# Token mixing in a four-stage network on one core: recurrence products moved to VectorE, key product split into high and low parts

## The reference

```python
xn = layer_norm(x, ln1_w, ln1_b); lx = time_shift(xn)
k = (xn * time_mix_k + lx * (1 - time_mix_k)) @ w_key      # v, r the same way
out = wkv(exp(time_decay), time_first, k, v)               # recurrence over time, per channel
x = x + out * sigmoid(r) @ w_output
xn2 = layer_norm(x, ln2_w, ln2_b); lx2 = time_shift(xn2)
fk = (xn2 * f_time_mix_k + lx2 * (1 - f_time_mix_k)) @ f_w_key      # 256 -> 1024
fr = (xn2 * f_time_mix_r + lx2 * (1 - f_time_mix_r)) @ f_w_recept
x = x + sigmoid(fr) * (square(relu(fk)) @ f_w_value)
```

## Time and profile before

| | |
|---|---|
| median of 3 runs | 1583.56 us (1581.69 to 1587.66) |
| the profiled execution: its own time | 1581.56 us |
| its span | 1579.8 us |
| PE busy | 1362.9 us (86%), 7400 matmuls |
| DVE busy | 924.3 us (59%) |
| ACT busy | 666.1 us (42%) |
| POOL busy | 680.1 us (43%) |
| mean granted clock of TensorE | 0.924 of full speed |

### The profile page before, as it was taken

One profiled execution on the slowest core, in us unless ns is written; L12 is line 12 of the kernel. 1 busy time (PEld: TensorE's weight loads), 2 busy tenths in 40 slices (PEclk: granted clock), 3 DMA queues, 4 the chain that ended last, 5 costly groups with the idle time before them and its releaser, 6 DMA issues. The chain is left out here.

```text
span 1579.8 us, 27682 instructions
## 1 busy us (share of the span) xinstructions
PE 1362.9 (86%) x7400; PEld 1108.9 (70%) x7401; DVE 924.3 (59%) x2098; ACT 666.1 (42%) x1497; POOL 680.1 (43%) x616
## 2 busy tenths in 40 slices
PE   4999975899999999336999999998937899999996
PEld 3998974778888888313665666576636788888885
DVE  5778776444444444277789888886145344444443
ACT  3576753222323333244557656764332223333332
POOL 3666743244445555213324323422132344455553
PEclk9899995899999999767999999999957999999998
DMA  6476662855553333420000000000017755533332
GB/s 207 182 245 230 214 250 82 281 136 132 128 134 54 58 57 54 128 82 1 1 14 28 14 13 27 27 14 27 14 41 229 236 131 130 134 54 60 54 54 37
DMA packets 100874, 157.84 MB, mean 100 GB/s; under 512 B 10256, under 2 KB 60688, under 8 KB 100816
## 3 DMA queue, kind: packets, MB, share of 16 engines
q1 hardware_dynamic: 73120, 118.67, 21.6%
q0 software_dynamic: 27264, 37.82, 14.5%
q10 hardware_dynamic: 432, 0.66, 0.2%
HBM read 95.89 MB, written 61.21 MB: 99 GB/s over the span
## 5 line engine op out<-in xcount | busy, mean ns | idle before, releaser
L1081 DVE TENSOR_TENSOR second_hT_lo<-bank,second_hT_hi 128x512 fp32r<-128x512 f32 x71 | 49.1, 692 | 170.3 <-ACT second_hT_hi L963 161.3
L1832 PE MATMUL bank<-b_xfk,b_fk 128*128 128x512 f32 x256 | 122.6, 637 | 27.1 <-DVE b_xfk L1595 16.7
L1081 DVE TENSOR_TENSOR first_hT_lo<-bank,first_hT_hi 128x512 fp32r<-128x512 f32 x71 | 49.1, 692 | 165.3 <-ACT first_hT_hi L963 156.3
L929 POOL DMA_INDIRECT out_x<-second_block_hot,second_add_token x53 | 84.0, 1585 | 127.6 <-DMA out_x<-second_block_hot,second_add_token 67.1
L929 POOL DMA_INDIRECT x_rows<-first_block_hot,first_add_token x53 | 84.0, 1584 | 125.8 <-DMA x_rows<-first_block_hot,first_add_token 67.9
L155 PE MATMUL bank<-second_ring,second_xT_hi 128*128 x284 | 120.8, 425 | 9.5 <-issue 7.4
L155 PE MATMUL bank<-first_ring,first_xT_hi 128*128 x284 | 120.5, 424 | 2.2 <-DVE first_xT_lo L1069 2.2
L1832 PEld LDWEIGHTS bank<-b_xfk,b_fk 128*128 128x128 f32 x256 | 51.3, 204 | 94.5 <-issue 64.8
L1753 PE MATMUL bank<-b_fv,b_hT 128*128 128x256 f32 x512 | 114.6, 383 | 0.0
L156 PE MATMUL bank<-first_ring,first_xT_hi 128*128 x284 | 113.5, 400 | 0.0
L157 PE MATMUL bank<-second_ring,second_xT_lo 128*128 x284 | 113.4, 399 | 0.0
(11 more groups left out here) (352 smaller groups left out, 3930.9 us busy)
## 6 DMA issues: line engine op xcount, KB each, us to landing
first_ring<-split_weights SPq DMA_DIRECT2D x96, 256.0 KB
second_ring<-split_weights SPq DMA_DIRECT2D x96, 256.0 KB
a_wraw<-in_L_ffn_w SPq DMA_DIRECT2D x24, 512.0 KB, 6.6
split_weights<-a_whi SPq DMA_DIRECT2D x24, 512.0 KB, 2.7
split_weights<-a_wlo SPq DMA_DIRECT2D x24, 512.0 KB, 4.1
normed_rows<-xg SPq DMA_DIRECT2D x16, 528.0 KB, 3.0
x_rows<-x SPq DMA_DIRECT2D x8, 512.0 KB, 7.2
x<-x_rows SPq DMA_DIRECT2D x8, 512.0 KB, 9.0
```

What stands on the lines that cost most here:

```text
L929: nc.gpsimd.indirect_dma_start(x_dram[:], bass.IndirectOffsetOnAxis(ap=add_token[q][:], axis=0), y[q], None, compute_op=ALU.add).then_inc( ...
L1081: nc.vector.tensor_tensor(hT_lo[par][:].rearrange("p k t -> p (k t)"), th_bank[par][:], hT_hi[par][:].rearrange("p k t -> p (k t)").bitcas ...
L1832: last = nc.tensor.matmul(xb_[m % 4][:], fk_s[:, i, m * P:(m + 1) * P], xfk[:, i, :], start=(i == 0), stop=(i == KC - 1))
```

## The change

- **Recurrence products.** dv = d2*v and num = rho*v leave POOL's queue for DVE's: dv behind `mix_channel` and the new `low_key`, ahead of `finish(b-1, 1)`; num between the two scans of the denominator and its add. `denominator` itself now stands behind `finish(b-1, 1)`, which so reads its bank straight behind the channel mix.
- **add_mixed** on POOL goes behind the router's rstd and waits for a semaphore that DVE raises just ahead of the reciprocal.
- **ACT's order.** `weights_of_step` is cut in two: the Relu pair stays ahead of `evacuate_xn2`, the Exp pair goes behind it. `carry(b+1)` goes from ahead of `hidden` to behind the router's norm.
- **mix_time** waits for the three projections one by one.
- **Prologue.** PE transposes both first norms ahead of any projection, ACT moves the second one out ahead of k and v.
- **Key product split.** f_w_key is loaded into part of b_hT, ACT rounds it to fk_hi, POOL subtracts to make fk_lo, once in the prologue. In each period ACT rounds xfk to xfk_hi (`high_key`), and DVE subtracts to make xfk_lo (`low_key`). Each chunk takes three products, 48 float32r MATMULs a period in place of 32: first the two with xfk_hi for chunks 0 to 3, then, once xfk_lo is there, the rest.

Queues and DMA: SP issues the same loads, with another destination for one.

```diff
-        fk_s = sb("fk", [P, KC, F])
+        fk_hi, fk_lo = sb("fk_hi", [P, KC, F], F32R), sb("fk_lo", [P, KC, F], F32R)
...
+        xfk_hi, xfk_lo = sb("xfk_hi", [P, KC, N], F32R), sb("xfk_lo", [P, KC, N], F32R)
         hT, fs = sb("hT", [P, FCH, N]), sb("fs", [P, 2, N])
+        fk_raw = hT[:, 0:KC * F // N, :].rearrange("p (k a) n -> p k (a n)", k=KC)
...
-            for dst, src in ((wo_s[:], w_output), (wf_s[:], f_w_recept), (fk_s[:], f_w_key), (fv_s[:], f_w_value)):
+            for dst, src in ((wo_s[:], w_output), (wf_s[:], f_w_recept), (fk_raw, f_w_key), (fv_s[:], f_w_value)):
...
-            def weights_of_step(b):
+            def gaps_of_step(b):
                 act.wait_ge(gam_ready, b + 1)
                 nc.scalar.activation(d1[:], gam[:], ACT.Relu).then_inc(expd, 1)
                 nc.scalar.activation(d2[:], gam[:], ACT.Relu, scale=-1.0).then_inc(expd, 1)
+            def weights_of_step(b):
                 act.wait_ge(expd, 6 * b + 1)
                 nc.scalar.activation(d1[:], d1[:], ACT.Exp, scale=-1.0).then_inc(expd, 1)
...
+            def high_key(b):
+                act.wait_ge(mix2_ready, 2 * b + 1)
+                nc.scalar.activation(xfk_hi[:], xfk[:], ACT.Copy).then_inc(xfk_hi_ready, 1)
...
             evacuate_xn(0)
             norm(1)
             act.wait_ge(prep, 3)
+            evacuate_xn(1)
             evacuate_k(0)
             evacuate_v(0)
-            evacuate_xn(1)
+            gaps_of_step(0)
             weights_of_step(0)
             evacuate_r(0)
             weight_of_first(0)
             carry(0)
             act.wait_ge(w_in, 64)
             nc.scalar.activation(wo_s[:], wo_s[:], ACT.Copy, scale=0.5).then_inc(halved, 1)
+            nc.scalar.activation(fk_hi[:], fk_raw, ACT.Copy).then_inc(fk_hi_ready, 1)
             nc.scalar.activation(fv_s[:], fv_s[:], ACT.Copy, scale=0.5).then_inc(halved, 1)
             def period(b):
                     row_exp(b - 2)
                 if has_next(b, 1):
                     evacuate_v(b + 1)
-                    weights_of_step(b + 1)
+                    gaps_of_step(b + 1)
                 evacuate_xn2(b)
                 if has_next(b, 1):
+                    weights_of_step(b + 1)
                     evacuate_r(b + 1)
+                high_key(b)
+                if has_next(b, 1):
                     weight_of_first(b + 1)
                 if has_before(b, 2):
                     row_finish(b - 2)
                 if has_next(b, 2):
                     norm(b + 2)
-                if has_next(b, 1):
-                    carry(b + 1)
                 hidden(b)
                 if has_next(b, 2):
                     evacuate_xn(b + 2)
                 receptance(b)
                 if has_before(b, 1):
                     route_norm(b - 1)
+                if has_next(b, 1):
+                    carry(b + 1)
+                if has_before(b, 1):
                     gate_rows(b - 1)
...
-            def decayed_value(b):
-                wait_apart(pool, kvr_evac, 6 * b + 4, passed["pool"])
-                wait_apart(pool, expd, 6 * b + 4, passed["pool"])
-                nc.gpsimd.tensor_tensor(dv[:], d2[:], v[:], ALU.mult).then_inc(dv_ready, 1)
-            def first_value(b):
-                wait_apart(pool, expd, 6 * b + 6, passed["pool"])
-                nc.gpsimd.tensor_tensor(num[:], rho[:], v[:], ALU.mult).then_inc(num_begun, 1)
...
-            decayed_value(0)
-            first_value(0)
+            pool.wait_ge(fk_hi_ready, 1)
+            nc.gpsimd.tensor_tensor(fk_lo[:], fk_raw, fk_hi[:].bitcast(F32), ALU.subtract).then_inc(fk_lo_ready, 1)
             def period(b):
                 rstd(mv2, shift2, own_2, var2_ready, rstd2_ready, b)
-                add_mixed(b)
                 if has_next(b, 2):
                     rstd_in(b + 2)
-                if has_next(b, 1):
-                    decayed_value(b + 1)
-                if has_next(b, 1):
-                    first_value(b + 1)
                 if has_before(b, 1):
                     add_channel(b - 1, 1)
                     rstd(mvg, shiftg, own_c, varg_ready, rstdg_ready, b - 1)
+                if has_next(b, 1):
+                    wait_apart(pool, num_ready, b + 2, passed["pool"])
+                add_mixed(b)
                 add_channel(b, 0)
...
-                for dst, m in outs:
+                for n, (dst, m) in enumerate(outs):
+                    if src is xnT:
+                        wait_count(dve, kvr_done, 6 * b - 4 + 2 * n)
                     for i in range(KC):
                         last = nc.vector.scalar_tensor_tensor(out=dst[:, i, :], in0=dT[:, i, :], scalar=vec[m][:, i:i + 1],
                                                               in1=src[:, i, 0:N], op0=ALU.mult, op1=ALU.add)
             def mix_time(b):
                 dve.wait_ge(t_emptied, round_xn(b) + 1)
-                wait_count(dve, kvr_done, 6 * b)
                 mixes(m_, xnT, ((xk, "time_mix_k"), (xv, "time_mix_v"), (xr, "time_mix_r")), b, mix_ready)
             def mix_channel(b):
                 dve.wait_ge(t_emptied, round_xn2(b) + 1)
                 mixes(m2, xn2T, ((xfk, "f_time_mix_k"), (xfr, "f_time_mix_r")), b, mix2_ready)
+            def low_key(b):
+                dve.wait_ge(xfk_hi_ready, b + 1)
+                nc.vector.tensor_tensor(xfk_lo[:], xfk[:], xfk_hi[:].bitcast(F32), ALU.subtract).then_inc(xfk_lo_ready, 1)
...
+            def decayed_value(b):
+                r_.round(b)
+                dve.wait_ge(kvr_evac, 6 * b + 4)
+                dve.wait_ge(expd, 6 * b + 4)
+                r_.link(nc.vector.tensor_tensor(dv[:], d2[:], v[:], ALU.mult))
             def denominator(b):
-                r_.round(b)
-                dve.wait_ge(expd, 6 * b + 4)
                 for i in range(KC):
                     last = nc.vector.tensor_tensor_scan(be[:, i, 1:N + 1], d1[:, i, :], d2[:, i, :], 0.0, ALU.mult, ALU.add)
+                dve.wait_ge(expd, 6 * b + 6)
+                nc.vector.tensor_tensor(num[:], rho[:], v[:], ALU.mult)
                 r_.link(last)
-                dve.wait_ge(expd, 6 * b + 6)
                 nc.vector.tensor_tensor(den[:], rho[:], be[:, :, 0:N], ALU.add)
             def numerator(b):
-                dve.wait_ge(dv_ready, b + 1)
                 for i in range(KC):
                     last = nc.vector.tensor_tensor_scan(al[:, i, 1:N + 1], d1[:, i, :], dv[:, i, :], 0.0, ALU.mult, ALU.add)
                 r_.link(last)
-                dve.wait_ge(num_begun, b + 1)
                 r_.link(nc.vector.tensor_tensor(num[:], num[:], al[:, :, 0:N], ALU.add))
             def quotient(b):
                 dve.wait_ge(kvr_evac, 6 * b + 6)
-                nc.vector.scalar_tensor_tensor(out=num[:], in0=sg[:], scalar=1.0, in1=num[:], op0=ALU.add, op1=ALU.mult)
+                r_.link(nc.vector.scalar_tensor_tensor(out=num[:], in0=sg[:], scalar=1.0, in1=num[:], op0=ALU.add, op1=ALU.mult))
+                dve.sem_inc(num_ready, 1)
                 r_.link(nc.vector.reciprocal(den[:], den[:]))
...
             mix_time(0)
             exponents(0)
             mix_time(1)
+            decayed_value(0)
             denominator(0)
             numerator(0)
...
                 if has_before(b, 2):
                     softmax_end(b - 2)
                 mix_channel(b)
+                low_key(b)
                 if has_next(b, 1):
-                    denominator(b + 1)
+                    decayed_value(b + 1)
                 if has_before(b, 1):
                     finish(b - 1, 1)
                 if has_next(b, 1):
+                    denominator(b + 1)
                     numerator(b + 1)
                 if has_before(b, 1):
                     route_statistics(b - 1)
                 token_product(xb_[2 + h], cut(hT, h), fv_s, FCH).then_inc(vk_done, 1)
             def key_products(b):
-                pe.wait_ge(mix2_ready, 2 * b + 1)
+                pe.wait_ge(xfk_hi_ready, b + 1)
                 if has_next(b, 1):
                     pe.wait_ge(kvr_evac, 6 * b + 12)
                 else:
                     pe.wait_ge(xb_ready, 2 * b + 2)
-                for m in range(FCH):
+                if static(b, 0):
+                    pe.wait_ge(fk_lo_ready, 1)
+                def key_product(m, w, src, start, stop):
+                    for i in range(KC):
+                        last = nc.tensor.matmul(xb_[m % 4][:], w[:, i, m * P:(m + 1) * P], src[:, i, :],
+                                                start=(start and i == 0), stop=(stop and i == KC - 1))
+                    return last
+                for m in range(4):
                     if m == 2:
                         wait_count(pe, sum_ready, 2 * b - 1)
                     if m == 3:
                         wait_count(pe, sum_ready, 2 * b)
+                    key_product(m, fk_hi, xfk_hi, True, False)
+                    key_product(m, fk_lo, xfk_hi, False, False)
```

(13 more changed lines are left out.)

7 lines of the change are left out of this document (4 added, 3 removed).

## The result

The changed kernel takes 1528.45 us (median of 4 runs, 1526.07 to 1529.51) against 1582.62 us for the kernel before in the same comparison: ratio 0.9653, 95% interval [0.9624, 0.9683]. I forecast 1538 us within 1530 to 1556. The direction was right, and the waits that I expected to go are gone, but the time lies 1.55 us under the low end, so the forecast is wrong: the gain is 54 us where I had 45. In one set of runs further down, pe_cut's, one execution of four took 4935.04 us for a reason that nothing here shows; the time given there is the median of the other three.

What follows compares the result with a forecast made beforehand. PE was the bound, though not a clean one: 4.4 of 54.1 us a period not work. Prologue 0, period 0 -7.2, periods 1 to 6 -35.9, last -2.3 sum to -45.4: 1536.2, or 1538 us against the median; range 1530 to 1556.

Steps and rivals of the forecast that it cites:

- All three losses of PE: At the key product: waits of 0.56 us for xfk and 2.13 for the bank, 1.7 of slow clock; all go.
- Rival B: DVE's reciprocal stands still beside add_mixed: 2.35 us on the loop, +13, total 1551 us; chance 0.15.
- C: Rival: ACT reaches `hidden` late by 3.5 us, PE waits 2.3 for b_hT, total 1556 us; chance 0.11.
- D: Rival: contention changes place, DVE's new two-input instructions stand still beside POOL; loop 53.7, total 1574 us; chance 0.04.
- E: Rival: key product runs at 1.2 GHz each period, 22.8 us for the 48, total up to 1629 us; chance 0.04.
- the loop: Inner period: a chain without PE, from dT through DVE, adds, norm2 and xn2T to dT, priced at 47.7 us.
- the 5.0: Loop term: from the second add to xb through statistics and POOL's rstd to norm2, 5.0 us.
- Period 0: -7.2 predicted: Key product of period 0 starts 4.9 us earlier and gains 2.3, with 1.7 of slow clock staying: 7.2.
- the 4 us for fk_lo: Prologue: POOL's fk_lo beside DVE's scans costs between 0 and 4.7 us; 4 taken.
- the rate of 0.7: Prologue: DVE loses 0.7 us for each us of POOL, from the eps scan's 1.67 to 2.35; gives 3.3.
- -4.4 + 2.5: Prologue: xk and xv without POOL's products beside them, 4.4 us less; dv and num on DVE, 2.5 more.
- the loop's 0.7: Inner periods: the loop's 47.7 us lies 0.7 over PE's own 47.0; without it the total is 2.5 less.

Runs made afterwards that it cites:

- pe_cut: Changed kernel without the 16 products of fk_lo with xfk_hi in each period: 1523.89 us, ratio 0.9636 to the kernel before.
- fklo_recip: Changed kernel with POOL's fk_lo held until DVE is at the first reciprocal: 1526.48 us, ratio 0.9654 to the kernel before.
- unsplit: Changed kernel with the key product in float32 again, 32 instructions, without fk_hi, fk_lo, high_key, low_key: 1547.67 us, ratio 0.9781.
- prologue_old: Changed kernel with PE transposing sequence 1's norm behind the projections of sequence 0 again: 1532.15 us, ratio 0.968.
- products_pool: Changed kernel with dv and num made on POOL again, all other parts kept: 1542.29 us, ratio 0.9747.
- bank_late: Changed kernel with the denominator ahead of finish(b-1, 1) on DVE again: 1563.7 us, ratio 0.9879.
- weights_first: Changed kernel with ACT's Exp pair ahead of the move of xn2T again: 1543.72 us, ratio 0.9762.
- add_old: Changed kernel with POOL's add_mixed back behind the channel norm's rstd, beside DVE's eps scans: 1532.36 us, ratio 0.9678.
- best: Changed kernel with fk_lo held until the first reciprocal and DVE's mix of sequence 1 behind the first quotient: 1525.62 us, ratio 0.9639.

## Why the prediction was wrong

**What held.** The key product: 11.4 us predicted, 11.39 measured. All three losses of PE went, as worked out from the order of DVE and ACT. Rival B is refuted: the reciprocal takes 6.55 us with add_mixed's 2.36 inside it, and in fklo_recip with 4.50 inside it. C did not come: there is no PE wait for b_hT. D did not: the three new DVE instructions take 1.2 us each. E did not in the inner periods: 1.00 of the clock there. And the loop is there, as pe_cut shows.

**The step that failed: the price of an inner period, 47.7 us by the loop and 47.0 by PE's own work, against 46.6 for both.** The loop's terms in period 3: dT to the end of `finish(b, 0)` 33.4 predicted and 33.4 measured (873.34 to 906.70); the adds to xb 1.4 and 1.2; from their end to norm2 5.0 and 4.2 (907.90 to 865.50 + 46.63); norm2 to xn2T 6.4 and 6.4; xn2T to dT 1.5 and 1.5. So the one large error is the 5.0. I took norm2's start at 886.86 as the end of the chain statistics, rstd, norm2. These are ACT, POOL and DVE there in the kernel before, and POOL and DVE in the changed one (DVE's first scan in the kernel before is in the earlier trace rows):

```profile
886.37 0.60 ACT L1374 ACTIVATE b_k<-bank 128x512 f32<-128x512 f32 x1 [1.12 <-PE bank L1765]
```
```profile
885.73 0.77 POOL L1509 TENSOR_TENSOR b_shift<-b_mv 128x4 f32<-128x4 f32 x1
```
```profile
865.15 0.32 POOL L1525 TENSOR_TENSOR b_shift<-b_mv 128x4 f32<-128x4 f32 x1
```
```profile
864.26 2.32 DVE L1625 TENSOR_TENSOR_SCAN b_eps<-b_ndecay,b_k 128x512 f32<-128x512 f32 x2
```

Both parts of the extra 0.8 us are waits for PE. ACT had first to move out the second half of k, for which it had waited for PE's projection, so norm2 started 0.36 us behind the end of b_shift (886.50). And b_shift, POOL's last instruction of the rstd, was itself 0.45 us longer: it ends with DVE's first scan for eps (885.28 + 1.23 = 886.51), which had waited for k and so for the same projection. In the changed kernel k is there in time, the scan starts at 864.26, and b_shift ends with it again, at 865.47. In `unsplit`, where PE is the bound, b_shift is back at 0.77 and ends with the scan (869.80 and 869.81); in the last period, which has no such scan, it takes 0.20. In the changed kernel norm2 waits for POOL's shift alone, 0.78 us after ACT is free: the 4.2 is the chain's own length, and `pe_cut`, where PE stands idle, has it too. Waits for PE were priced into a loop that was to be without PE.

With that the loop no longer lies over PE's own work. This takes 46.63 us and not 47.0, because I took the wait ahead of the key product at its bracket, 0.56 us. The bracket counts from the modelled end of the value product. From start to start the same 32 instructions took 7.63 us (893.91 to 901.54) where they now take 6.72 (871.66 to 878.38), so the wait had cost 0.91.

```profile
893.91 7.07 PE L1753 MATMUL bank<-b_fv,b_hT 128*128 128x256 f32 x32
```

Periods 2 to 5 take 186.53 us where I had 190.3, 3.8 us: 2.3 of them are the loop, 1.5 PE's own work. PE's own work gives 0.3 more in period 6 and 0.4 in period 1. Together that is 4.5 of the 6.7 us by which 52.05 exceeds 45.4.

**Period 1.** I gave it 47.0 us like the rest, and it took 44.84: 2.2 us more of gain, 1.8 beside the 0.4 just counted. It has no gate product (1.71 us from 905.33 to 907.04 in period 3). PE makes that product for the sequence two before the one whose output product it has just made, and here there is none yet. A term left out by taking an inner period for all.

**Period 0: -7.2 predicted, -5.30 measured.** Start of the key product against the output product's: 27.02 us before, 23.23 after, 3.8 earlier and not 4.9, since the output product itself ran more of its time at 1.2 GHz (6.08 us from start to start against 4.99, at a granted clock of 0.57 against 0.70). Its key product had 2.5 us of slow clock and not 1.7: 738.60 to 752.53 is 13.93, against 11.39 in period 3, and from 738.6 to 744.6 the granted clock was 0.51.

**Prologue: 0 predicted, -1.82 measured.** The 4 us for fk_lo were taken between two bounds, by no row, and met the 4.07 of fklo_recip by luck. The Trainium skill (SBUF — State Buffer, Who interferes with whom) has the port as a lock held for a whole instruction, which would take nearly all of fk_lo's 4.63 us. The trace sides with that and not with the rate of 0.7 that I had read from the eps scan: the two al scans went from 2.33 to 6.64 us, 4.31 lost. The eps scan fits the lock as well, since it came 0.54 us into the add's 2.35 and lost 1.67 of the 1.81 that were left. POOL's products gone and DVE's added came out as predicted, -1.8 for -4.4 + 2.5: from dT of sequence 1 to the end of gT it is 25.58 us in the kernel before (689.82 to 715.40) and 23.81 in fklo_recip (688.39 to 712.20). What I had too low is the way to that dT:

```profile
687.15 1.22 DVE L1597 TENSOR_TENSOR b_dT<-b_xnT 128x1024 f32<-128x1024 f32 x1
```

It starts 27.91 us into the stage where it was 32.27, 4.4 earlier and not 2.4. By prologue_old, where it is 30.56, the order of PE and ACT gives 2.65 of that and the single waits of `mix_time` 1.7. I had given the whole to the early transposes, at 2.4. So -4.4 - 1.8 + 4.3 = -1.8.

**Tail: -2.3 predicted, -3.57 measured.** The key product gave 2.4; the value product ahead of it gave 1.0 more: 7.6 us between starts against 8.6 (1100.80 to the key product's 1109.38), with less of it at the slow clock (granted 0.88 over it against 0.80).

**The range.** Its low end, 1530, already had three savings together: the loop's 0.7 gone (2.5 us), no slow clock in period 0 (1.7), fk_lo hidden (4). Only the first came. What carried the time below it were terms for which I gave no bound: PE's own 47.0, period 1's gate product, the prologue's waits, the tail. The price of an inner period was multiplied by five, and its error with it. The last step counts as well: I added 2.0 us because the profiled execution of the kernel before lay under its median, but the changed kernel's, 1529.51, lies 1.06 over its own. So 3.1 of the 9.55 us between 1538 and 1528.45 are differences between executions and no mechanism.

## What to carry to other kernels

Before a stretch of the trace is priced into a loop, look at what released its last instruction: the 5.0 us ended behind two instructions, one on ACT and one on POOL, that had been held up by the very engine that the loop was to leave out. Read a wait of PE from start to start and not from its bracket. When several edits clear one engine's waits, their worth doesn't add up: here the split is worth 0 alone and 15 us last, the place of one DVE instruction 34, and four single undoings (unsplit, products_pool, bank_late, weights_first) lengthen the stage by 15.3, 11.3, 34.1 and 12.9 us, 73.6 together, where the whole change shortened it by 52.8. Look through the first and the last periods for instructions they lack, and place POOL's large instructions beside a DVE instruction with one input.

## What the runs showed of the hardware

- DVE instructions with two inputs in SBUF and POOL's `tensor_tensor` exclude each other for a whole instruction. In period 3 POOL's add wants to start at 880.80 and takes 1.93 us rather than the 1.28 it takes at 860.25: it waits 0.65 us, about the rest of DVE's first scan. The second scan then waits: the pair takes 3.39 rather than 2.33. In add_old both sides show it too (POOL 3.31 for 2.36, DVE 3.32 for 1.42). It holds for POOL's smallest instructions as well: b_shift, 128 x 4, takes 0.20 us with no scan beside it and 0.77 to 0.83 in the inner periods of the kernel before, where it ends with DVE's scan.
- The fp32 reciprocal is free of it, from either side: 6.55 us with 2.36 or 4.50 us of POOL's large instructions inside, and with neither (add_old).
- A float32r product of 128 x 128 by 128 x 512 starts every 0.233 us, a float32 instruction of the same shape every 0.43, and a float32 product is two of those: 0.70 for three against 0.86. The Trainium skill (FP8 and Floating Point Precision, TensorE Precision Notes) has true float32 as four passes through the array. An estimate from that, three quarters of 13.7, is 10.3 us for the 48; the measured 11.4 decides.
- The moment at which the clock rises behind an idle stretch moved by up to 1.4 us between runs in which PE's work up to there was the same (project_k(0): 3.97 us in unsplit, 4.04 in the changed kernel, 4.16 in fklo_recip, 5.35 in best). Such a shift is as large as some of the edits. In the kernel before, too, a wait of 2.13 us ahead of chunk 3 was followed by 10.4 us for 20 instructions in period 3, and in period 5, at a granted clock of 1.00, by 8.7 us (1017.25 to 1025.94).
